# Maxima of the row scores put into a row by VectorE's 32x32 transposes instead of TensorE's transpose and ScalarE's copy

## The chip, the cores and the metric

One core of a Trainium2 chip runs the whole program. The metric is the device time of one launch in microseconds (us), given as the median of several runs; beside it there is one profiled execution, whose trace the rows below come from.

## The reference

A layer with x of 8 x 256 tokens and 512 channels. Cut to what matters here:

```
xn = layernorm(x)
c_q, c_kv = xn @ Wq_down, xn @ Wkv_down              # 64 latent columns
q_c, k_c, v_c = (c_q @ Wq_up, c_kv @ Wk_up, c_kv @ Wv_up), 128 heads of 4
q_r, k_r = xn @ Wq_rope (128 heads of 64), xn @ Wk_rope (64, shared by the heads)
scores = (q_c . k_c + q_r . k_r) / sqrt(68)          # per batch and head, 256 x 256
s = (softmax(scores) @ v_c) @ Wo
g = silu(ffn(xn))                                    # low-rank feed-forward net
out = x + s * g
```

## The kernel before

The program has three stages: projections of the input (`project_inputs`), attention (`attention`) and the end with the feed-forward net (`finish`). Each engine has a program of its own; the order of work on each is written out by hand, and semaphores tie the engines together.

The attention stage runs over 16 groups of heads (G2); a group has STEPS = 16 steps, four pairs of batches (NBP) times four launches of two heads (NS). Group 0 and group 15 are written out, the 14 between are a loop (`groups`). Each engine's `body(at, k)` holds what it does in step k, for steps that lie several places apart in the pipeline:

- `project` (L999, TensorE) makes the rope part of the queries of step k in the PSUM tile pj; ScalarE copies its rounded high part into slot1 (L848), VectorE subtracts to get the low part into slot2 (L916, once per head of the pair: it reads pj at partition 0 and then at 64, and writes slot2 at 64) and copies the rest of slot2 (L920, written at partition 0).
- `row_scores` (L985, TensorE) computes scores of step k - 1 with queries on the partitions, into the PSUM tile sx, in two halves, one per head; after each half VectorE takes the maxima over the keys (`maxima`, L906) into mx, four columns each. After two steps 16 columns of mx are full.
- The maxima are needed as a row: they enter the real scores as one more row of the contraction, slot1[KC]. So every second step (odd k) `transpose_maxima` (L952, TensorE) transposes the 16 columns into the PSUM tile sx, ScalarE copies them to mrow (L864), and SyncE moves mrow into slot1 by DMA (`max_rows`, L713).
- `scores` (L968, TensorE) computes the scores of step k - 4 and k - 3 with keys on the partitions, into st; ScalarE takes the exponentials (L887) into probs; `values` (L944) multiplies them with the values, in 32-column tiles of TensorE, for two steps at a time in every odd step.

SyncE's queue issues, in an odd step, first the row (L713, after a wait on mrow_ready) and then the content of step k (`load_content`: L697 and twice L701), the latent parts of queries and keys that row scores of step k read one step later. L697 waits for GpSimd's copy into k1 (L782). A wait and what is queued behind it on one engine go in the order of the code. In the last group's extra step k = 17 the transpose comes behind the last row scores, and ScalarE's queue issues the row.

TensorE's order in an odd step is: values of two steps, the transpose of the maxima, the second half of the scores of step k - 4, row scores of step k - 1 (first half), the projection of step k, row scores (second half). In an even step it is: both halves of scores of one step, row scores, the first half of the next scores, projection, row scores.

Of the kernel before, what the change touches and what calls it, by code (L numbers as in the profile page):

```python
# [30 lines left out]
NE = 13  # L31
# [31 lines left out]
class AttentionSemaphores:  # L63


    def __init__(self, sem, ct_lo, w_ready):
        self.ct_lo, self.w_ready = ct_lo, w_ready
        self.proj_done = sem("proj_done")
        self.ct_in = [sem(f"ct_in{s}") for s in range(NS)]
        self.st_done = sem("st_done")  # L70
        self.av_done = sem("av_done")
        self.o_evac = sem("o_evac")
        self.o_stored = sem("o_stored")
        self.k_ready = sem("k_ready")
        self.ql_done = sem("ql_done")


# [138 lines left out]
def project_inputs(nc, sb, sem, passed, x_tok, wq_down, wkv_down, wk_rope, a1T, a3T, wv_up, wq_up, wk_up, v_dram, c_dram, s_dram,  # L216
# [10 lines left out]
    with ctx:  # L227
# [372 lines left out]

        return sync, gpsimd, scalar, vector, tensor, store_tile, empty_tile, raise_up


def attention(nc, sb, sem, at_sems, passed, xh, xl, kc, krlh, c_in, probs, w_stage, wh, wl, wq_rope, w_staged, w_hi,
              w_ready, ident, v_dram, c_dram, o_dram, stored, c_loaded, ct_hi, ct_lo, ct_copy, pre, store_tile, empty_tile, raise_up):

# [6 lines left out]
    with ctx:  # L613
# [5 lines left out]
        vx = sb(ctx, "vx", [128, NS, 4, PH, 32])  # L619
        mx = sb(ctx, "mx", [128, 2, 16])  # L620
        mrow = sb(ctx, "mrow", [16, 2, 128], F32R)
        o_sb = sb(ctx, "o_sb", [128, S])
# [18 lines left out]
        smax_done = sem("smax_done")  # L641
        red_done = sem("red_done")
        mt_done = sem("mt_done")
        mrow_ready = sem("mrow_ready")
# [64 lines left out]
        def sync(sp, head, tail):  # L709
            def max_rows(at, k):  # L710
                p = (k // 2) % 2
                hold(sp, passed, mrow_ready, at.g * (STEPS // 2) + k // 2 + 1)
                sp.dma_start(slot1[KC:KC + 1, 2 * p:2 * p + 2, :, :, :].bitcast(F32),  # L713
                             mrow[:, p, :].bitcast(F32)).then_inc(mrow_in[p], 16)

# [55 lines left out]
        def gpsimd(pool, head, tail):  # L771
# [45 lines left out]
            def refill(g, s):  # L817

                hold(pool, passed, w_hi, g * NS + s + 1)
                nc.gpsimd.tensor_tensor(wl[:, s], w_stage[:, s % 2], wh[:, s], ALU.subtract).then_inc(w_ready, 1)  # L820

            nc.gpsimd.memset(vx[:, :, :, :, :], 0.0).then_inc(vx_filled, 1)
            pool.wait_ge(vx_filled, 1)
# [12 lines left out]
        def scalar(act, head, tail):  # L836
# [4 lines left out]
            def body(at, k):  # L841
# [14 lines left out]
                if s == 1 and at.live(k - 6):  # L856
# [3 lines left out]
                    nc.scalar.activation(o_sb[:, :], ob[:, 0, :], ACT.Copy).then_inc(o_evac, 1)  # L860
                if k % 2 and at.live(k - 3) and k - 3 < STEPS:
                    p = (k - 3) // 2
                    act.wait_ge(mt_done, at.g * (STEPS // 2) + p + 1)
                    nc.scalar.activation(mrow[:, p % 2, :], sx[0:16, 0, 0:128], ACT.Copy).then_inc(mrow_ready, 1)  # L864
                    if at.last and k > STEPS:
                        act.wait_ge(mrow_ready, at.g * (STEPS // 2) + p + 1)
                        act.dma_start(slot1[KC:KC + 1, 2 * (p % 2):2 * (p % 2) + 2, :, :, :].bitcast(F32),
                                      mrow[:, p % 2, :].bitcast(F32)).then_inc(mrow_in[p % 2], 16)
                if at.live(k - 4) and k - 4 < STEPS:
# [26 lines left out]
        def vector(dve, head, tail):  # L896
            def content_lo(parity, t):
                c = content[parity % 2]
                dve.wait_ge(ct_hi, t + 1)
                nc.vector.tensor_tensor(c[:, 2, :], c_in[64:128, :], c[:, 0, :], ALU.subtract).then_inc(ct_lo, 1)  # L900

            def maxima(at, k, half):
                p, i = (k // 2) % 2, k % 2
                dve.wait_ge(smax_done, 2 * at.step(k) + half + 1)
                lo = 8 * i + 4 * half
                nc.vector.tensor_reduce(mx[:, p, lo:lo + 4], sx[:, :, :].rearrange("p a (b k) -> p (a b) k", b=2),  # L906
                                        axis=AX.X, op=ALU.max).then_inc(red_done, 1)

            def body(at, k):
                if at.live(k - 2) and k - 2 < STEPS:  # L910
                    maxima(at, k - 2, 1)
                if at.live(k - 1) and k <= STEPS:
                    s = (k - 1) % NS
                    for e in range(PH):
                        dve.wait_ge(qh_done, 2 * at.step(k) + e - 1)
                        nc.vector.tensor_tensor(slot2[64:128, s, e, :, :],  # L916
                                                pj[64 * e:64 * e + 64, :].rearrange("p (a n) -> p a n", a=2),
                                                slot1[0:64, s, e, :, :], ALU.subtract).then_inc(ql_done, 1)
                if at.live(k - 1) and k <= STEPS:
                    nc.vector.tensor_copy(slot2[0:64, s], slot1[0:64, s]).then_inc(s2_done, 1)  # L920
                    maxima(at, k - 1, 0)
                if k % NS == 2 and k < STEPS and at.live(k + 2):
                    content_lo(k // NS + 1, at.turn(k) + 1)

            groups(dve, body, head, tail)

        def tensor(pe, head, tail):
# [21 lines left out]

            def transpose_maxima(at, k):  # L950
                pe.wait_ge(red_done, 2 * at.step(k) + 4)
                nc.tensor.transpose(sx[0:16, 0, 0:128], mx[:, (k // 2) % 2, :], ident[:, :]).then_inc(mt_done, 1)  # L952

            def scores(at, k, kt):
                s, v = k % NS, at.step(k)
                b = 2 * ((k // NS) % NBP)
                if kt == 0 and k % 2 == 0:
                    if at.first and k == 0:
                        pe.wait_ge(pre.krl_done, NC)
                        pe.wait_ge(pre.krh_copied, 16 * NC)  # L960
                    pe.wait_ge(mrow_in[s // 2], 16 * (at.turn(k) + 1))
                if at.live(k - 1):
# [9 lines left out]
            def row_scores(at, k, half):  # L972
# [3 lines left out]
                if not half:  # L976
                    pe.wait_ge(qh_done, 2 * v + 2)
                    pe.wait_ge(ct_in[s], 48 * (at.turn(k) + 1))
                    if at.first and k < 2:
                        pe.wait_ge(k_ready, k + 1)  # L980
                    if k % 2 == 0 and at.live(k - 2):
                        pe.wait_ge(mrow_ready, at.g * (STEPS // 2) + k // 2)
                for h in range(2):
# [19 lines left out]
            def body(at, k):  # L1003
# [4 lines left out]
                if k % 2 and not ending:  # L1008
                    if at.live(k - 7):
                        values(at, k - 7, 2)  # L1010
                        values(at, k - 6, 0)
                    if at.live(k - 3) and k - 3 < STEPS:
                        transpose_maxima(at, k - 3)
                if ending and k > STEPS + 1:
# [14 lines left out]
                if at.live(k - 1) and k <= STEPS:  # L1029
                    row_scores(at, k - 1, 1)  # L1030
                if ending and k == STEPS + 1:
                    transpose_maxima(at, k - 3)

# [5 lines left out]
def finish(nc, sb, at_sems, passed, sem, x_tok, xh, xl, lora, lora_raw, mk, ident, stored, s_dram, o_dram, r_dram, wo, w1qT, b1T, w3qT, b3T,  # L1039
# [504 lines left out]
    def tensor_tail(pe, k):  # L1544

        if k == 17:
            pe.wait_ge(w13_lo, 4)
            pe.wait_ge(sl_done, NC)
            pe.wait_ge(at_sems.ql_done, 2 * NS * NT)
            wide(pe, 0, 0)  # L1550

# [136 lines left out]
```

## Time and profile before

| what | us |
|---|---|
| median of 3 runs | 1972.71 (1969.94 to 1976.02) |
| profiled execution | 1970.24 |
| its span | 1968.1 |
| TensorE busy | 1932.3 |
| VectorE busy | 1391.0 |
| ScalarE busy | 1055.4 |
| GpSimd busy | 476.2 |

The attention stage takes some 1,700 us of the span. The granted clock of TensorE is 0.998 of full in the mean. To read the profile: busy time of a pipelined engine says little of what sets the end, so the timelines of single pairs of steps, where each event's start and end stand beside the others', are read along with the chain of waits.

### The profile page before, as it was taken

Reading aid. Unit: us, or ns where it says so; the run is one execution under the profiler, and the core shown is the slowest. Engines: PE = TensorE matmul, PEld = TensorE weight load, DVE = VectorE, ACT = ScalarE, POOL = GpSimd, SP = SyncE. Lnnn points to the kernel's source line nnn. Section 1 sums busy time; section 2 is a strip of 40 time slices with the busy share of each in tenths; the row PEclk is TensorE's granted clock in tenths of the full one; section 3 lists DMA queues with packets and bytes.
Section 4 is the critical chain, followed back from the end, with each engine's and each line's share of the span. In section 5 each row is a group of like instructions: output and inputs, shape, how many; then the busy total and the mean of one; then the engine's idle time right before and its main releaser. Section 6 shows DMA issues by size and latency. Waiting matters only on the chain.

```text
span 1968.1 us, 37690 instructions
## 1 busy us (share of the span) xinstructions
PE 1932.3 (98%) x12464; PEld 1504.6 (76%) x12464; DVE 1391.0 (71%) x1642; ACT 1055.4 (54%) x1542; POOL 476.2 (24%) x792
## 2 busy tenths in 40 slices
PE   7899999999999999999999999999999999998999
PEld 5777877777787777778777777877787777775676
DVE  8688767676776767676776767677776767687655
ACT  5656555555555555555555555555555555564222
POOL 5323121212212121212121222222131312112221
PEclk9999999999999999999999999999999999999999
DMA  7612111111212121212112121212121211234331
GB/s 240 206 38 59 31 41 38 38 37 34 45 27 50 28 50 25 51 28 43 34 39 40 35 40 34 43 28 50 29 46 29 49 28 37 46 82 132 107 102 54
DMA packets 132875, 107.97 MB, mean 55 GB/s; under 512 B 52350, under 2 KB 96430, under 8 KB 132766
## 3 DMA queue, kind: packets, MB, share of 16 engines
q1 hardware_dynamic: 132798, 107.38, 23.2%
q8 instruction: 26, 0.43, 0.1%
q14 instruction: 19, 0.16, 0.0%
q10 hardware_dynamic: 32, 0.01, 0.0%
HBM read 52.80 MB, written 27.26 MB: 41 GB/s over the span
## 4 chain that ended last, share of the span: by engine, by line
PE 94%; DVE 3%; SPq 1%; issue 1%; DMA 1%; ACT 0%; POOL 0%; DVEq 0%; ACTq 0%; POOLq 0%
PE pj L999 35%; PE st L968 24%; PE sx L985 12%; PE ob L944 12%; PE ap L1597 2%; PE sx L952 1%; PE yp L1631 1%; PE zp L1631 1%; PE gp L1538 1%; PE zp L1584 1%; PE gp L1563 1%; PE tp L565 0%; DVE mx L906 0%; PE gp L1539 0%; PE gp L1540 0%
## 5 line engine op out<-in xcount | busy, mean ns | idle before, releaser
L906 DVE TENSOR_REDUCE mx<-sx 128x4 f32<-128x1024 f32 x512 | 626.9, 1224 | 427.8 <-PE sx L985 410.0
L887 ACT ACTIVATE probs<-st 128x1024 f32<-128x1024 f32 x512 | 513.1, 1026 | 165.2 <-PE st L968 164.5
L848 ACT ACTIVATE slot<-pj 64x512 fp32r<-64x512 f32 x512 | 303.4, 592 | 424.0 <-PE pj L999 417.7
L782 POOL CAST k<-kc 64x512 fp32r<-64x512 f32 x256 | 168.1, 657 | 1055.1 <-PE st L968 1054.7
L968 PE MATMUL st<-slot,k 89*128 89x512 f32 x1024 | 417.8, 408 | 4.1 <-DMA slot<-mrow 4.1
L968 PE MATMUL st<-slot,krlh 128*128 128x512 f32 x1024 | 408.3, 399 | 0.0
L999 PE MATMUL pj<-xh,wh 128*128 128x512 f32 x1024 | 401.4, 392 | 0.9 <-DVE slot L916 0.8
L999 PE MATMUL pj<-xh,wl 128*128 128x512 f32 x1024 | 400.6, 391 | 0.0
L999 PE MATMUL pj<-xl,wh 128*128 128x512 f32 x1024 | 399.4, 390 | 0.0
L916 DVE TENSOR_TENSOR slot<-pj,slot 64x512 fp32r<-64x512 f32 x512 | 353.1, 690 | 17.4 <-ACT slot L848 1.3
L985 PEld LDWEIGHTS sx<-k,slot 88*128 88x128 f32 x2048 | 314.1, 190 | 50.4 <-issue 4.1
L985 PE MATMUL sx<-k,slot 88*128 88x256 f32 x2048 | 327.7, 282 | 3.5 <-DMA slot<-kx 1.3
L944 PE MATMUL ob<-probs,vx 128*32 128x256 f32 x4096 | 247.8, 382 | 1.1 <-ACT probs L887 1.1
L999 PEld LDWEIGHTS pj<-xh,wl 128*128 128x128 f32 x1024 | 192.2, 188 | 42.7
L999 PEld LDWEIGHTS pj<-xh,wh 128*128 128x128 f32 x1024 | 192.6, 188 | 38.3 <-issue 1.2
L999 PEld LDWEIGHTS pj<-xl,wh 128*128 128x128 f32 x1024 | 192.8, 188 | 38.1
L968 PEld LDWEIGHTS st<-slot,k 89*128 89x128 f32 x1024 | 196.1, 192 | 33.0 <-DMA slot<-mrow 4.6
L968 PEld LDWEIGHTS st<-slot,krlh 128*128 128x128 f32 x1024 | 195.7, 191 | 29.5
L944 PEld LDWEIGHTS ob<-probs,vx 128*32 128x32 f32 x4096 | 119.9, 109 | 85.0 <-ACT probs L887 2.3
L920 DVE CAST slot<-slot 64x1024 fp32r<-64x1024 f32 x256 | 176.6, 690 | 7.9
L820 POOL TENSOR_TENSOR wl<-w_stage,wh 128x512 fp32r<-128x512 f32 x60 | 77.2, 1287 | 57.6 <-ACT wh L892 57.6
L864 ACT ACTIVATE mrow<-sx 16x128 fp32r<-16x128 f32 x128 | 33.1, 259 | 88.1 <-PE sx L952 88.1
(180 smaller groups left out, 1300.8 us busy)
## 6 DMA issues: line engine op xcount, KB each, us to landing
w_stage<-in_Wq_rope SPq DMA_DIRECT2D x64, 256.0 KB, 3.1
c_scratch<-stage SPq DMA_DIRECT2D x32, 256.0 KB, 3.1
c_in<-c_scratch SPq DMA_DIRECT2D x128, 64.0 KB, 1.9
o_scratch<-o_sb SPq DMA_DIRECT2D x128, 64.0 KB, 2.1
k<-kc SPq DMA_DIRECT2D x128, 48.0 KB
slot<-kc SPq DMA_DIRECT2D x256, 24.0 KB
k<-kx SPq DMA_DIRECT2D x128, 48.0 KB
slot<-kx SPq DMA_DIRECT2D x256, 24.0 KB
```

What stands on the lines that cost most here:

```text
L782: nc.gpsimd.tensor_copy(k1[0:64, s, :, :].rearrange("p a n -> p (a n)"), krh[:, bp * CH:(bp + 1) * CH]).then_inc(k_ready, 1)
L820: nc.gpsimd.tensor_tensor(wl[:, s], w_stage[:, s % 2], wh[:, s], ALU.subtract).then_inc(w_ready, 1)
L848: nc.scalar.activation(slot1[0:64, (k - 1) % NS, e, :, :], pj[64 * e:64 * e + 64, :].rearrange("p (a n) -> p a n", a=2), ACT.Copy).then_in ...
L887: nc.scalar.activation(probs[:, k % NS, kt], st[:, kt], ACT.Exp, scale=SCALE).then_inc(exp_done, 1)
L906: nc.vector.tensor_reduce(mx[:, p, lo:lo + 4], sx[:, :, :].rearrange("p a (b k) -> p (a b) k", b=2), axis=AX.X, op=ALU.max).then_inc(red_d ...
L916: nc.vector.tensor_tensor(slot2[64:128, s, e, :, :], pj[64 * e:64 * e + 64, :].rearrange("p (a n) -> p a n", a=2), slot1[0:64, s, e, :, :] ...
L920: nc.vector.tensor_copy(slot2[0:64, s], slot1[0:64, s]).then_inc(s2_done, 1)
L944: last = nc.tensor.matmul(ob[j:j + 32, 0, :], vx[:, s, 2 * h + kt, e, :], probs[:, s, kt, h, e * S:(e + 1) * S], start=(s == 0 and kt == 0 ...
L968: last = nc.tensor.matmul(st[:, kt, h, :].rearrange("p (e n) -> p e n", e=PH), kk, q[0:n_rows, s, :, h, :], start=(n == 0), stop=(n == 1))
L985: last = nc.tensor.matmul(sx[:, h, qt * S:(qt + 1) * S], slot1[0:KC, s, half, h, qt * 128:qt * 128 + 128], k1[0:KC, s, h, :], start=True, ...
L999: last = nc.tensor.matmul(pj[:, :], w[:, s, c, :], xx[:, c, ts], start=(c == 0 and n == 0), stop=(c == KD - 1 and n == 2))
L1597: last = nc.tensor.matmul(ap[i % 2][:, :], o[:, k, i * 128:(i + 1) * 128], w[:, k, :], start=(k == 0 and n == 0), stop=(k == KD - 1 and n ...
```

## The change

VectorE does the turning. A function `max_row` waits for both steps' maxima and issues four transposes of 32x32 from mx (partitions 32j to 32j + 31) to mrow (partitions 0 to 31, columns from 32j), in SBUF. mx is widened to 32 columns for each of its two buffers, zeroed once by GpSimd, and of the rounded type that the copy gave the row before; mrow gets 32 partitions, of which 16 are sent. TensorE's transpose, ScalarE's copy and TensorE's wait for that copy are gone. SyncE waits for the fourth transpose. In the extra step ScalarE's queue still issues the row. Two waits are added that took their place in the order from the transpose before: TensorE waits for the last staged tile before the first scores, and for all maxima before it uses the banks in the last stage.

```diff
-        mx = sb(ctx, "mx", [128, 2, 16])
-        mrow = sb(ctx, "mrow", [16, 2, 128], F32R)
+        mx = sb(ctx, "mx", [128, 2, 32], F32R)
+        mrow = sb(ctx, "mrow", [32, 2, 128])
...
             def max_rows(at, k):
                 p = (k // 2) % 2
-                hold(sp, passed, mrow_ready, at.g * (STEPS // 2) + k // 2 + 1)
+                hold(sp, passed, mrow_ready, 4 * (at.g * (STEPS // 2) + k // 2 + 1))
                 sp.dma_start(slot1[KC:KC + 1, 2 * p:2 * p + 2, :, :, :].bitcast(F32),
-                             mrow[:, p, :].bitcast(F32)).then_inc(mrow_in[p], 16)
+                             mrow[0:16, p, :]).then_inc(mrow_in[p], 16)
...
+            nc.gpsimd.memset(mx[:, :, :].bitcast(F32), 0.0).then_inc(mx_zeroed, 1)
             nc.gpsimd.memset(vx[:, :, :, :, :], 0.0).then_inc(vx_filled, 1)
...
-                if k % 2 and at.live(k - 3) and k - 3 < STEPS:
+                if at.last and k == STEPS + 1:
                     p = (k - 3) // 2
-                    act.wait_ge(mt_done, at.g * (STEPS // 2) + p + 1)
-                    nc.scalar.activation(mrow[:, p % 2, :], sx[0:16, 0, 0:128], ACT.Copy).then_inc(mrow_ready, 1)
...
+            def max_row(at, k):
+
+                dve.wait_ge(red_done, 2 * at.step(k) + 4)
+                for j in range(4):
+                    nc.vector.transpose(mrow[:, (k // 2) % 2, 32 * j:32 * j + 32],
+                                        mx[32 * j:32 * j + 32, (k // 2) % 2, :].bitcast(F32)).then_inc(mrow_ready, 1)
+
             def body(at, k):
                 if at.live(k - 2) and k - 2 < STEPS:
                     maxima(at, k - 2, 1)
+                if k == STEPS + 1:
+                    max_row(at, k - 3)
...
                                                 slot1[0:64, s, e, :, :], ALU.subtract).then_inc(ql_done, 1)
+                if k % 2 and at.live(k - 3) and k < STEPS:
+                    max_row(at, k - 3)
                 if at.live(k - 1) and k <= STEPS:
                     nc.vector.tensor_copy(slot2[0:64, s], slot1[0:64, s]).then_inc(s2_done, 1)
...
-            def transpose_maxima(at, k):
-                pe.wait_ge(red_done, 2 * at.step(k) + 4)
-                nc.tensor.transpose(sx[0:16, 0, 0:128], mx[:, (k // 2) % 2, :], ident[:, :]).then_inc(mt_done, 1)
...
+                        wait_tile(pe, NC * NE - 1)
...
-                    if k % 2 == 0 and at.live(k - 2):
-                        pe.wait_ge(mrow_ready, at.g * (STEPS // 2) + k // 2)
...
+            pe.wait_ge(at_sems.red_done, 2 * NS * NT)
```

On TensorE, in an odd step of the loop (ob is the values' tile, st the scores', sx the row scores'), before:

```order
L944 MATMUL ob<-probs,vx 32x256 [waits vx_ready,exp_done]
L944 MATMUL ob<-probs,vx 32x256 x15
L951 ISA
L952 MATMUL sx<-ident,mx 16x128 [waits red_done]
L968 MATMUL st<-slot,k 128x512 [waits exp_done]
L968 MATMUL st<-slot,krlh 128x512
```

and with the change:

```order
L956 MATMUL ob<-probs,vx 32x256 [waits vx_ready,exp_done]
L956 MATMUL ob<-probs,vx 32x256 x15
L977 MATMUL st<-slot,k 128x512 [waits exp_done]
L977 MATMUL st<-slot,krlh 128x512
L977 MATMUL st<-slot,k 128x512
```

The transpose is gone, and scores follow the values directly.

On VectorE, in an odd step of the loop (the slot of the subtractions and of the copy is slot2), before:

```order
L906 TENSOR_REDUCE mx<-sx 128x4 [waits smax_done]
L915 ISA
L916 TENSOR_TENSOR slot<-pj,slot 64x512 [waits qh_done] x2
L920 COPY slot<-slot 64x1024
L904 REGISTER_ALU
L906 TENSOR_REDUCE mx<-sx 128x4 [waits smax_done]
```

and with the change:

```order
L907 TENSOR_REDUCE mx<-sx 128x4 [waits smax_done]
L925 ISA
L926 TENSOR_TENSOR slot<-pj,slot 64x512 [waits qh_done] x2
L912 REGISTER_ALU
L914 STREAM_TRANSPOSE mrow<-mx 32x32 [waits red_done]
L914 STREAM_TRANSPOSE mrow<-mx 32x32 x3
L932 COPY slot<-slot 64x1024
```

Four transposes stand between the subtractions and the copy; the maxima that the first of them waits for are the ones ahead of the subtractions.

## Rows read from the trace of the kernel before

**Rows 1.** page, busy time of each engine, share of the span, instructions

```profile
PE 1932.3 (98%) x12464; PEld 1504.6 (76%) x12464; DVE 1391.0 (71%) x1642; ACT 1055.4 (54%) x1542; POOL 476.2 (24%) x792
```

**Rows 2.** chain of waits, 937 to 951 us: start us, us, engine and tile

```profile
937.21 0.21 PE sx L952
...
941.57 0.48 PE sx L985 x4
...
950.45 0.21 PE sx L952
```

**Rows 3.** timeline of TensorE: start us, us, engine, line, operation

```profile
937.14 0.28 PE L952 MATMUL sx<-ident,mx 128*16 128x128 f32 x1
...
937.49 0.40 PE L968 MATMUL st<-slot,krlh 128*128 128x512 f32 x1
...
1784.05 1.07 PE L944 MATMUL ob<-probs,vx 128*32 128x256 f32 x16
1785.05 0.50 PE L968 MATMUL st<-slot,k 89*128 89x512 f32 x1
1785.39 0.40 PE L968 MATMUL st<-slot,krlh 128*128 128x512 f32 x1
```

**Rows 4.** timelines of ScalarE, GpSimd and SyncE's queue (SPq)

```profile
937.46 0.27 ACT L864 ACTIVATE mrow<-sx 16x128 fp32r<-16x128 f32 x1 [1.34 <-PE sx L952]
...
937.83 0.59 SPq L713 DMA_DIRECT2D slot<-mrow  x1
...
938.54 0.70 POOL L782 CAST k<-kc 64x512 fp32r<-64x512 f32 x1 [2.43 <-PE st L968]
...
939.35 0.80 SPq L697 DMA_DIRECT2D k<-kc  x1
...
1708.24 0.61 SPq L713 DMA_DIRECT2D slot<-mrow  x1
1708.97 0.80 SPq L697 DMA_DIRECT2D k<-kx  x1
```

**Rows 5.** timeline of VectorE

```profile
1.52 0.17 DVE L519 TENSOR_REDUCE mk<-ident 128x1 f32<-128x16 f32 x1 [1.52 <-POOL ident L362]
...
7.46 0.38 DVE L470 BATCH_NORM_AGGREGATE mv<-stats 128x2 f32<-128x6 f32 x4
...
936.64 1.41 DVE L916 TENSOR_TENSOR slot<-pj,slot 64x512 fp32r<-64x512 f32 x2
938.08 0.69 DVE L920 CAST slot<-slot 64x1024 fp32r<-64x1024 f32 x1
938.88 1.23 DVE L906 TENSOR_REDUCE mx<-sx 128x4 f32<-128x1024 f32 x1
```

**Rows 6.** two lines of VectorE: duration ns minimum, median, maximum

```profile
L916 DVE TENSOR_TENSOR slot<-pj,slot x512: 683/690/697, 76.8 to 1767.2; 64x512 fp32r<-64x512 f32 x171
...
L470 DVE BATCH_NORM_AGGREGATE mv<-stats x16: 148/150/184, 7.5 to 50.7; 128x2 f32<-128x6 f32 x16
```

**Rows 7.** timeline of TensorE and its weight loads (PEld)

```profile
931.00 0.39 PE L968 MATMUL st<-slot,k 89*128 89x512 f32 x1
...
943.58 0.61 PEld L985 LDWEIGHTS sx<-k,slot 88*128 88x128 f32 x4
...
944.24 0.40 PE L968 MATMUL st<-slot,k 89*128 89x512 f32 x1
...
1740.01 0.54 PEld L985 LDWEIGHTS sx<-k,slot 88*128 88x128 f32 x4 [0.48 <-issue]
...
1740.59 0.40 PE L968 MATMUL st<-slot,k 89*128 89x512 f32 x1
```

**Rows 8.** stretches: us, busy of PE, PEld, DVE, ACT, POOL, clock, DMA share, GB/s

```profile
929.65:929.70 0.05, 0.05 (x2) 0.05 (x1) 0.05 (x1) 0.00 (x0) 0.00 (x0) 1.00 0.14 41
...
1739.50:1739.55 0.05, 0.05 (x1) 0.03 (x1) 0.05 (x1) 0.05 (x1) 0.00 (x0) 1.00 0.10 41
```

**Rows 9.** what TensorE's transpose (L952) waited for: us, times

```profile
  DVE mx L906: 8.6, 10
```

More of the change, by code:

```diff
@@ L75, in __init__ @@
         self.ql_done = sem("ql_done")
+        self.red_done = sem("red_done")
 def hold(eng, passed, semaphore, value):
@@ L599, in tensor @@
                     raise_up(pe, c, n)
-        return sync, gpsimd, scalar, vector, tensor, store_tile, empty_tile, raise_up
+        return sync, gpsimd, scalar, vector, tensor, store_tile, empty_tile, raise_up, wait_tile
 def attention(nc, sb, sem, at_sems, passed, xh, xl, kc, krlh, c_in, probs, w_stage, wh, wl, wq_rope, w_staged, w_hi,
-              w_ready, ident, v_dram, c_dram, o_dram, stored, c_loaded, ct_hi, ct_lo, ct_copy, pre, store_tile, empty_tile, raise_up):
+              w_ready, ident, v_dram, c_dram, o_dram, stored, c_loaded, ct_hi, ct_lo, ct_copy, pre, store_tile, empty_tile, raise_up, wait_tile):
     KC = 64 + 3 * HD * PH
@@ L641, in attention @@
         smax_done = sem("smax_done")
-        red_done = sem("red_done")
-        mt_done = sem("mt_done")
+        red_done = at_sems.red_done
+        mx_zeroed = sem("mx_zeroed")
         mrow_ready = sem("mrow_ready")
@@ L860, in body @@
                     nc.scalar.activation(o_sb[:, :], ob[:, 0, :], ACT.Copy).then_inc(o_evac, 1)
-                if k % 2 and at.live(k - 3) and k - 3 < STEPS:
+                if at.last and k == STEPS + 1:
                     p = (k - 3) // 2
-                    act.wait_ge(mt_done, at.g * (STEPS // 2) + p + 1)
-                    nc.scalar.activation(mrow[:, p % 2, :], sx[0:16, 0, 0:128], ACT.Copy).then_inc(mrow_ready, 1)
[L865 to L868, printed above, removed]
+                    act.wait_ge(mrow_ready, 4 * (at.g * (STEPS // 2) + p + 1))
+                    act.dma_start(slot1[KC:KC + 1, 2 * (p % 2):2 * (p % 2) + 2, :, :, :].bitcast(F32),
+                                  mrow[0:16, p % 2, :]).then_inc(mrow_in[p % 2], 16)
                 if at.live(k - 4) and k - 4 < STEPS:
@@ L903, in maxima @@
                 p, i = (k // 2) % 2, k % 2
+                if at.first and k == 0:
+                    dve.wait_ge(mx_zeroed, 1)
                 dve.wait_ge(smax_done, 2 * at.step(k) + half + 1)
@@ L1011, in body @@
                         values(at, k - 6, 0)
-                    if at.live(k - 3) and k - 3 < STEPS:
-                        transpose_maxima(at, k - 3)
                 if ending and k > STEPS + 1:
@@ L1030, in body @@
                     row_scores(at, k - 1, 1)
-                if ending and k == STEPS + 1:
-                    transpose_maxima(at, k - 3)
             groups(pe, body, head, tail)
```

## The prediction

> **What bounds the kernel now.** I read the page's busy shares first: TensorE is busy for 98% of the span, VectorE for 71% [rows 1]. The chain of waits gives the transpose of the maxima 0.21 us in each pair of steps [rows 2]. I then read one pair on every engine, because a queue that is off the chain can hold a margin that no total shows. A pair takes 13.24 us (937.21 to 950.45 [rows 2]), and there are 128 (16 groups of 16 steps). The reader should see in the timelines which event ends last before each TensorE group: mostly TensorE's own work, but with hardly anything spare at one place, the content that SyncE issues right behind the row (mrow).
>
> **TensorE: the transpose and its slot.** In the pair at 937 us the transpose starts at 937.14, right behind the column-tiled value matmuls, and the second score matmul starts at 937.49, 0.35 us later. At the program's end a value group of the same kind is followed by a score group with no transpose between: first score matmul 1785.05, second 1785.39, 0.34 us later [rows 3]. So the slot is no gain: the transpose's short weight load and its columns run where the first score matmul would otherwise stand waiting for its 128 columns of weights. I take 0.01 us a pair, over 120 pairs **-1.2 us**. The bounds are that 0.01 and the chain's 0.21. The Trainium skill has a rule for the gap itself (TensorEngine Tiling (Array Packing), Key Properties): a change of tiling mode drains TensorE. By it the gap belongs to the value matmuls and stays, and the trace agrees with its 0.34 us.
>
> **ScalarE.** The copy of the row goes (0.27 us [rows 4]). ScalarE is not on the path between maxima and scores at that place: its next work waits for score matmuls. Nothing is gained. If that cover were gone, 0.27 us a pair would be.
>
> **VectorE: four transposes.** They stand between the two subtractions (L916) and the copy (L920), in odd steps. No row shows such a transpose. The length of one: a reduction of 128x16 takes 0.17 us [rows 5]; 16 more columns at the pace of VectorE's long rows (690 ns for 512 columns less 170 ns for 16, over 496: about 1.05 ns a column) give 0.19 us. Lower end 0.15 (the 128x6 aggregation, 150 ns), upper end 0.22 (0.19 plus 32 columns once more, should the block be filled before it is emptied). The pitch: four aggregations in a row take 0.38 us where one takes 0.150, so they overlap by about 0.07 each. Two L916 take 1.41 us at 690 ns each, so they don't overlap but lie 0.03 us apart [rows 5, 6]. What differs: the aggregations all start at partition 0, while L916 reads its PSUM tile at partition 0 and then at 64, and L920 behind it goes back to an output at partition 0 and starts 0.03 us after the end (936.64 + 1.41 = 938.05, then 938.08). The four transposes read mx at partitions 0, 32, 64, 96 in turn, so I price them as L916: 4 x 0.19 + 3 x 0.03 = **0.85 us** from the first's start to the last's end. Ends: 4 x 0.15 + 0.09 = 0.69 and 4 x 0.22 + 0.09 = 0.97. If they overlap as the aggregations do: 4 x (0.19 - 0.07) + 0.07 = 0.55. The Trainium skill states this as a rule (VectorE: DVE Perf Modes, Two Vector instructions with no wait between them): an instruction whose operand starts in another group of 32 partitions than the one used before is held, and "starts only when every earlier Vector instruction has finished". The rows of L916 and L920 agree with it; the rule speaks against this change.
>
> TensorE waits next for VectorE at the second row scores (941.57 [rows 2]), behind 12 projection matmuls that start as before, since the subtractions keep their place. The maxima for them now end at 938.88 + 1.23 = 940.11; with 0.85 + 0.03 more in the queue, and no wait for matmuls left before them, they start at 938.08 + 0.88 + 0.69 + 0.03 = 939.68 and end at 940.91. The projection hides the four; if that cover were gone, all of 0.88 us a pair would be on the path.
>
> **SyncE's queue: what the later row pushes.** The row is now stored with the fourth transpose. Before: ScalarE's copy ends at 937.73 and SyncE issues the row at 937.83, 0.10 us later; the next issue (L697, content of step k) then waits until GpSimd's copy ends at 939.24 and starts at 939.35 [rows 4]. Now: transposes from 938.08 to 938.93, issue at 939.03. A row and a content issue back to back start 0.73 us apart (1708.24 to 1708.97), so L697 comes at 939.76: **0.41 us late**. The three content issues, their DMAs and what waits for them all move with it. The limit on the transposes for no delay here is 0.85 - 0.41 = 0.44 us.
>
> Who waits for the content: row scores of step k, in the next step. Does it have 0.41 us to spare? In the tail, content issued at 1735.78 comes last: its final packets are at 1739.55, the weight load goes at 1740.01 (0.46 later), and the score matmul behind the four row scores at 1740.59, 0.58 after that [rows 7, 8]. In the pair at 937 us the weight load goes at 943.58; next to matmuls that start in steps of 0.23 us it is not early, and the matmul behind is at 944.24. Late content at 943.58 would give 944.16, so 0.08 us is spare. Moved by 0.41: 943.99 + 0.58 = 944.57, **0.33 us lost**. In the pair before it the last packet is at 929.70 and the matmul behind at 931.00: 929.70 + 0.46 + 0.41 + 0.58 = 931.15, **0.15 us lost** [rows 7, 8]. The two kinds alternate; the mean is 0.24, over 120 pairs **+28.8 us**. 128 pairs exist; the ones in which the queue is busy with loads of the last stage are left out.
>
> **Head and tail.** In the first steps TensorE waits at the transpose for the maxima, 8.6 us in 10 waits of the whole run [rows 9], the bound of that gain; most of it returns at the projection, which waits for the subtractions behind the same maxima. At the end VectorE's queue is the chain, and two calls of 0.85 us stand in it, +1.7 us at most; the last one takes the place of the transpose and the copy (0.28 + 0.27). I take both together as 0. The zeroing of mx on GpSimd (once) and the wait for the last staged tile before the first scores come long before they are needed.
>
> **The sum.** -1.2 + 28.8 = +27.6 us. The profiled execution took 1970.24 us for a span of 1968.1; with the sum 1997.8. The median of the runs lies 2.5 us above the profiled execution, so I forecast 2000.3 us. With 0.69 us for the four the delay is 0.25: 0.17 and 0.00 us lost, mean 0.085, +10 us: 1982. With 0.97 the delay is 0.53: 0.45 and 0.27, mean 0.36, +43 us: 2015.
>
> **The rivals.**
> - *Hidden after all.* The transposes overlap (0.55 us): the delay is 0.11, of which 0.08 is spare in one kind and more in the other, 0.02 us a pair in the mean: about 1972.7 - 1.2 + 2 = 1973.5 us. For it: the aggregations. Against it: L916, L920. Likewise if content lands sooner once its issue is not tied to GpSimd. Chance 0.20.
> - *Faster: the slot is worth something.* If the drain vanished with the transpose, each pair would win between 0.01 and 0.21 us; it decides for a gain as soon as the delay of the queue is under 0.08 us, which asks for transposes under 0.52 us. At 0.11 us x 128 the time is 1958.6 us. The Trainium skill (TensorE: Matmul & The Clock Gate, PE-mode transpose) puts such a transpose at about 275 ns in a kernel's context, and the row has 0.28; by that figure the removal would give 128 x 0.275 = 35 us. Against it stand the two distances of 0.35 and 0.34 us. Chance 0.07.
> - *Much slower: a transpose costs as much as an operation of 256 columns.* Half of L916's 0.69 us, 0.35, gives 4 x 0.35 + 0.09 = 1.49 us, a delay of 1.05 and 0.88 us a pair: 2077 us. Nothing in the rows for it but that the form is unknown. Chance 0.05.
>
> **The numbers.** A measurement of this kernel can tell 0.3%, 5.9 us, from no change. My forecast has 0.68. It is slower by over 5.9 us in all of its range. With the third rival slower is 0.73, from which I move 0.01 for a sum near the bound: 0.72. Same has the first rival and a little of the others, 0.22; faster 0.06. The range: the forecast's own is 1982 to 2015; for 8 in 10 it must reach the first rival, so it goes down to 1970.
>
> **What would show it.** Right: four transposes of about 0.19 us, each starting 0.03 us after the last; SyncE issues the row 0.10 us after the fourth and content 0.73 us behind that; the weight load of the row scores in even steps shows idle time that ends with the landing of content; the pair grows from 13.24 to about 13.47 us; first to second score matmul 0.34 us. Wrong: transposes that overlap; content still issued 0.1 us after GpSimd's copy; a pair of 13.1 us or less; a new wait at the second row scores, or at the scores for the row itself.

## The result, and the profile after

The changed kernel takes **2018.6 us** (median of 4 runs, 2017.08 to 2019.04) against 1973.07 us (1969.94 to 1976.02) for the kernel before, now with a fourth run: a ratio of **1.023** (95% interval 1.0215 to 1.0248), 45.5 us slower. The forecast was 2000.3 us, slower, with a range from 1970 to 2015. The direction and the mechanism were right; the loss was 45.5 us instead of 27.6, and the time lies outside the range. The profiled execution took 2018.73 us for a span of 2016.6.

The page of the changed kernel: busy shares (line 1 answers to [rows 1]), the chain by engine, and the group of the new transposes:

```profile
PE 1959.7 (97%) x12336; PEld 1496.5 (74%) x12336; DVE 1490.7 (74%) x2154; ACT 1027.8 (51%) x1414; POOL 523.4 (26%) x793
...
PE 65%; DVE 11%; DMA 9%; SPq 8%; issue 7%; ACT 1%; DVEq 0%; ACTq 0%
...
L914 DVE STREAM_TRANSPOSE mrow<-mx 32x32 f32<-32x32 f32 x512 | 102.8, 201 | 15.9
```

VectorE gained 99.7 us of busy time, close to the 102.8 us of the transposes. TensorE is still at 97%, a share that says nothing of the cause. The second line does: in the chain that ended last, SyncE's queue now has 8% and the DMAs 9%. Before the change the same line of the page was

```profile
PE 94%; DVE 3%; SPq 1%; issue 1%; DMA 1%; ACT 0%; POOL 0%; DVEq 0%; ACTq 0%; POOLq 0%
```

The chain through one odd step and into the next, in the loop (start, length, what):

```profile
963.22 0.21 DVE mrow L914
963.47 0.05 issue
963.51 0.59 SPq L714
...
964.30 0.80 SPq L698
965.10 0.05 issue
965.15 0.68 SPq L702
965.83 0.04 issue
965.87 2.58 DMA slot<-kc
968.46 0.14 issue
968.59 0.71 PE sx L992 x4
```

Read it downwards: the fourth transpose (the others stand ahead of it in the chain), issue of the row, issue of the content right behind, its DMA, and then the row scores of the next step. That is the path the prediction named. The row's own DMA isn't in it.

Two pairs of steps side by side. The timelines of TensorE (matmuls, then weight loads), where each x32 row is a pair's start:

```profile
932.50 1.93 PE L956 MATMUL ob<-probs,vx 128*32 128x256 f32 x32
946.15 1.93 PE L956 MATMUL ob<-probs,vx 128*32 128x256 f32 x32
948.01 0.50 PE L977 MATMUL st<-slot,k 89*128 89x512 f32 x1
948.35 0.40 PE L977 MATMUL st<-slot,krlh 128*128 128x512 f32 x1
...
955.44 0.40 PE L977 MATMUL st<-slot,k 89*128 89x512 f32 x1
```

```profile
941.29 0.54 PEld L992 LDWEIGHTS sx<-k,slot 88*128 88x128 f32 x4 [0.60 <-DMA slot<-kx]
...
954.86 0.54 PEld L992 LDWEIGHTS sx<-k,slot 88*128 88x128 f32 x4 [0.53 <-issue]
```

and those of VectorE, then of SyncE's queue:

```profile
947.51 1.41 DVE L926 TENSOR_TENSOR slot<-pj,slot 64x512 fp32r<-64x512 f32 x2
948.95 0.89 DVE L914 STREAM_TRANSPOSE mrow<-mx 32x32 f32<-32x32 f32 x4
949.87 0.69 DVE L932 CAST slot<-slot 64x1024 fp32r<-64x1024 f32 x1
```

```profile
936.30 0.59 SPq L714 DMA_DIRECT2D slot<-mrow  x1
937.08 0.81 SPq L698 DMA_DIRECT2D k<-kx  x1
...
949.94 0.57 SPq L714 DMA_DIRECT2D slot<-mrow  x1
950.70 0.75 SPq L698 DMA_DIRECT2D k<-kc  x1
```

The transposes run from 948.95 to 949.84, 2.80 to 3.69 us after the pair's start. The row is issued at 949.94, the content at 950.70, 4.55 us after the start; in the pair before, 4.58 (937.08 - 932.50). Before the change it was 4.07: content at 939.35 [rows 4], in the pair that starts at 935.28 (timeline of the kernel before, TensorE):

```profile
935.28 1.93 PE L944 MATMUL ob<-probs,vx 128*32 128x256 f32 x32
```

The weight load of the even step's row scores now ends an idle time of 0.53 to 0.60 us, where [rows 7] show one at 943.58 that starts in step. The load at 954.86 has the next score matmul behind it at 955.44, 0.58 us later as in the prediction, and first and second score matmul are 0.34 us apart (948.01, 948.35), with no transpose ahead of them. The mean pair between 300 and 1650 us, from the starts of the first and the last value group there over their number (about 100), grew from **13.234 to 13.604 us** (forecast about 13.47): 0.370 x 128 = 47 us, against 48.5 us of span (2016.6 less 1968.1). The time is lost evenly in the loop.

### The profile page after: what moved, and what is told of

Its sections match the earlier page's. It is cut to its first block, busy times and chain, and to the rows that moved or that the text cites. A ratio compares the mean times of both kernels' runs of the same rounds, so it can differ in the third digit from the quotient of the medians.

```text
span 2016.6 us, 37584 instructions
## 1 busy us (share of the span) xinstructions
PE 1959.7 (97%) x12336; PEld 1496.5 (74%) x12336; DVE 1490.7 (74%) x2154; ACT 1027.8 (51%) x1414; POOL 523.4 (26%) x793
## 4 chain that ended last, share of the span: by engine, by line
PE 65%; DVE 11%; DMA 9%; SPq 8%; issue 7%; ACT 1%; DVEq 0%; ACTq 0%
PE pj L1006 25%; PE st L977 15%; PE sx L992 10%; PE ob L956 5%; DVE slot L926 5%; DMA slot<-kx 4%; DMA slot<-kc 4%; SPq L698 3%; DVE mrow L914 2%; SPq L702 2%; PE ap L1601 2%; SPq L714 2%; DVE mx L907 1%; PE yp L1635 1%; PE zp L1635 1%
## 5 line engine op out<-in xcount | busy, mean ns | idle before, releaser
L907 DVE TENSOR_REDUCE mx<-sx 128x4 fp32r<-128x1024 f32 x512 | 626.9, 1224 | 339.4 <-PE sx L992 331.1
L783 POOL CAST k<-kc 64x512 fp32r<-64x512 f32 x256 | 155.7, 608 | 1039.9 <-PE st L977 1039.5
L992 PEld LDWEIGHTS sx<-k,slot 88*128 88x128 f32 x2048 | 305.1, 190 | 109.7 <-issue 63.9
L992 PE MATMUL sx<-k,slot 88*128 88x256 f32 x2048 | 337.5, 287 | 25.6 <-DMA slot<-kc 8.6
L802 POOL COPY vx<-v_it 128x32 f32<-128x32 f32 x256 | 112.0, 438 | 22.9 <-POOL kc L816 8.9
L914 DVE STREAM_TRANSPOSE mrow<-mx 32x32 f32<-32x32 f32 x512 | 102.8, 201 | 15.9
```

The costliest lines, as they stand in the source:

```text
L783: nc.gpsimd.tensor_copy(k1[0:64, s, :, :].rearrange("p a n -> p (a n)"), krh[:, bp * CH:(bp + 1) * CH]).then_inc(k_ready, 1)
L802: nc.gpsimd.tensor_copy(vx[:, s, :, :, 4 * s:4 * s + 4], v_it[:, (kk // NS) % 2].rearrange("p n (e s r) -> p n e s r", e=PH, s=NS)[:, :, : ...
L914: nc.vector.transpose(mrow[:, (k // 2) % 2, 32 * j:32 * j + 32], mx[32 * j:32 * j + 32, (k // 2) % 2, :].bitcast(F32)).then_inc(mrow_ready, 1)
L992: last = nc.tensor.matmul(sx[:, h, qt * S:(qt + 1) * S], slot1[0:KC, s, half, h, qt * 128:qt * 128 + 128], k1[0:KC, s, h, :], start=True, ...
```

## The experiments

Each kernel is the changed one with the edit shown, unless it says otherwise, and is compared with the kernel before on the same chip (1970.5 us for three, two, same_part and row_on_act; 1970.7 for load_alone, slot_alone and first; 1969.7 for copy_first and act_again). Times after the start of a pair are from the timelines of five pairs (880 to 1010 us); pairs are means as above.

**Fewer transposes.** Three, and then two; mrow is zeroed once, and the rest of the row stays zero. ScalarE's wait in the extra step is lowered likewise.

```diff
-                hold(sp, passed, mrow_ready, 4 * (at.g * (STEPS // 2) + k // 2 + 1))
+                hold(sp, passed, mrow_ready, 3 * (at.g * (STEPS // 2) + k // 2 + 1))
...
+            nc.gpsimd.memset(mrow[:, :, :], 0.0).then_inc(mx_zeroed, 1)
...
-                for j in range(4):
+                for j in range(3):
...
```

> Three transposes instead of four (the last 32 queries' maxima are left out of the row, which keeps zeros there). Theory (the row comes late by the length of the transposes, and SyncE issues the content behind it): three take 3 x 0.20 + 2 x 0.03 = 0.66 us instead of the 0.89 of the changed kernel, the content's delay falls from 0.50 to 0.27 us, the loss of a pair from about 0.41 to 0.18 us: about 1995 us. Rival (each transpose costs the path its own time, wherever it stands): three quarters of 45.5 us are left: 2007 us.

> Two transposes instead of four (half of the maxima are left out of the row). Theory: 0.43 us in a row, a delay of 0.04 us, which is spare in both kinds of pair: within 3 us of the kernel before, about 1973 us. Rival (each transpose costs the path its own time): half of 45.5 us is left, 1996 us.

The edit shown is that of three; two has 2 in place of 3. Three: 1989.2 us, ratio 1.0095 (1.0076 to 1.0113). Two: 1967.5 us, 0.9986 (0.9974 to 0.9997). Two transposes cost nothing that can be measured, the third 22 us, the fourth 29 us (2018.6 less 1989.2; 27 us by the two ratios, as the change was measured beside another set of runs of the kernel before). That is a limit, not a load: the content is issued 4.10, 4.33 and 4.56 us after the pair's start with two, three and four, and the pair takes 13.206, 13.373 and 13.604 us. Both versions came out about 6 us under what I expected. Of that, 2.6 us is the kernel before, which ran at 1970.5 us here and at 1973.07 beside the change; most of the rest is the slot of TensorE's transpose, 4.4 us by the run slot_alone below, which the expectations hardly counted. Fewer transposes did not lower VectorE's busy time: 1490 us with three and 1492 with two, against 1491 with four, because its copy into slot2 starts earlier and then takes longer (last section). So the time of the program falls here while VectorE's load stays.

**The same number, but overlapping (same_part).** All four read the first block of mx, so that they take the same number of instructions, semaphores and columns but never change the partitions they read.

```diff
-                                        mx[32 * j:32 * j + 32, (k // 2) % 2, :].bitcast(F32)).then_inc(mrow_ready, 1)
+                                        mx[0:32, (k // 2) % 2, :].bitcast(F32)).then_inc(mrow_ready, 1)
```

> All four transposes read mx at partitions 0 to 31, so that the row holds the first 32 queries' maxima four times. Theory (they stand one behind the other because each reads at another group of partitions than the one before): now they overlap by 0.07 to 0.08 us each, four take 4 x 0.12 + 0.08 = 0.56 us, the content's delay is 0.17 us and the loss of a pair about 0.08 us: about 1983 us. Rival (a transpose never overlaps with the next, whatever it reads): four still take 0.89 us and the time stays at 2018 us.

2000.2 us, ratio 1.0145 (1.0126 to 1.0163), faster than the change by about 18 us, but 17 us above my figure. The line's own durations (min/median/max ns), then one pair on VectorE, GpSimd and SyncE:

```profile
L914 DVE STREAM_TRANSPOSE mrow<-mx x512: 156/157/200, 90.3 to 1802.5; 32x32 f32<-32x32 f32 x171
```

```profile
953.82 0.48 DVE L914 STREAM_TRANSPOSE mrow<-mx 32x32 f32<-32x32 f32 x4
954.23 0.64 DVE L932 CAST slot<-slot 64x1024 fp32r<-64x1024 f32 x1
...
954.25 1.10 POOL L783 CAST k<-kc 64x512 fp32r<-64x512 f32 x1 [2.39 <-PE st L977]
...
954.39 0.59 SPq L714 DMA_DIRECT2D slot<-mrow  x1
955.45 0.81 SPq L698 DMA_DIRECT2D k<-kc  x1
```

Four transposes in 0.48 us: the first of four takes 200 ns, the others 157, and each of these starts 0.06 us before the end of the one ahead; the copy behind starts 0.07 us before they end. So the 0.89 us of the change comes from the partitions it reads. The Trainium skill (VectorE: DVE Perf Modes, Two Vector instructions with no wait between them) says that an instruction whose operand starts in another group of 32 partitions than the one used before is held until all earlier ones have finished; here the trace agrees, with 0.03 us between two transposes in the change and an overlap of 0.06 us in this kernel. The surprise is in the last rows. The row is issued 0.42 us earlier than in the change, yet the content only 0.12 us (4.44 against 4.56 us after the pair's start): it waits for GpSimd's copy into k1, which took 1.10 us instead of 0.61 and ended at 955.35, 0.48 us after VectorE's copy (954.87). With the transposes short, that copy of VectorE's falls onto GpSimd's. This kernel has a second reason for late content, and its pair still fits the first: content at 4.44, pair 13.476.

**VectorE's load without the wait (load_alone).** The kernel before, with four transposes of a spare tile at the place of the new ones; nobody waits for them.

```diff
+            nc.gpsimd.memset(spare[:, :], 0.0)
...
+                if k % 2 and at.live(k - 3) and k < STEPS:
...
+                    for j in range(4):
+                        nc.vector.transpose(spare_row[:, 32 * j:32 * j + 32], spare[32 * j:32 * j + 32, :])
```

> The kernel before, with four further transposes of a spare tile on VectorE at the place where the change has them; nobody waits for them. Theory (VectorE's load as such is hidden): TensorE waits for VectorE only behind the projection, within 3 us of the kernel before. Rival (the four transposes hold up TensorE through the second maxima, or take a port from GpSimd): slower, up to the 45.5 us of the change.

1970.0 us, ratio 0.9998 (0.9989 to 1.0007); the pair is 13.238 us. Transposes of 0.2 us, 508 of them, cost nothing on VectorE, later copy and later second maxima included. They take 0.84 us for four and not 0.89, with 0.01 us between two and not 0.03; the content is issued 3.97 us after the pair's start.

**The slot alone (slot_alone).** The kernel before without TensorE's transpose, except in the last step; ScalarE waits for the maxima instead and copies what lies in sx.

```diff
-                    act.wait_ge(mt_done, at.g * (STEPS // 2) + p + 1)
...
+                        act.wait_ge(red_done, 2 * at.step(k - 3) + 4)
...
-                    if at.live(k - 3) and k - 3 < STEPS:
-                        transpose_maxima(at, k - 3)
```

> The kernel before without TensorE's transpose in all steps but the last (ScalarE copies what stands in the row scores' tile, so that the row is not the maxima). Theory (the slot of the transpose is filled by the weight load that the first score matmul would wait for anyway): 0.01 us a pair, 1 to 2 us in all, not to be told from no change; the second score matmul still comes 0.34 us after the start of the first. Rival (the slot is worth its columns, 0.11 us, or the 0.21 us of the chain): 14 to 27 us faster, 1946 to 1959 us.

1965.8 us, ratio 0.9976 (0.9967 to 0.9984), 4.8 us faster. From the value group to the row scores the kernel before takes 2.92 us (timeline, TensorE):

```profile
948.52 1.93 PE L944 MATMUL ob<-probs,vx 128*32 128x256 f32 x32
...
951.44 0.64 PE L985 MATMUL sx<-k,slot 88*128 88x256 f32 x4
```

and this kernel 2.90, with 0.34 us between first and second score matmul (947.06 - 946.72), as in the change:

```profile
944.86 1.93 PE L947 MATMUL ob<-probs,vx 128*32 128x256 f32 x32
...
946.72 0.50 PE L971 MATMUL st<-slot,k 89*128 89x512 f32 x1
947.06 0.40 PE L971 MATMUL st<-slot,krlh 128*128 128x512 f32 x1
...
947.76 0.63 PE L988 MATMUL sx<-k,slot 88*128 88x256 f32 x4
```

The pair is 13.200 us, 0.034 us shorter. So the slot is worth 0.034 x 128 = 4.4 us: more than my 0.01 a pair, and an eighth of the 0.28 us its row shows. The Trainium skill (TensorE: Matmul & The Clock Gate, PE-mode transpose) gives about 275 ns for a transpose on TensorE in one kernel's context, beside a figure for 128x128 bf16; this one has 16 columns of four bytes, and its row shows 0.28 us. Taken as a saving, that would have been 35 us in this run; it isn't.

**The row on another queue (row_on_act, and again as act_again).** All of the change, but in every odd step ScalarE's queue issues the row, and SyncE's queue issues content only.

```diff
-                if k % 2 and at.live(k - 3) and not (at.last and k > STEPS):
-                    max_rows(at, k - 3)
...
-                if at.last and k == STEPS + 1:
+                if k % 2 and at.live(k - 3) and k - 3 < STEPS:
                     p = (k - 3) // 2
```

> ScalarE's queue issues the row in every odd step, SyncE's queue no longer waits for it. The transposes stay. Theory (the loss is all in SyncE's queue behind the row): content goes right behind GpSimd's copy again, the pair takes 13.24 us and the program about 1972 us, at most 5 us more should ScalarE's issue of about 0.6 us delay an exponential that TensorE waits for. Rival (VectorE's longer work holds up TensorE): the time stays near 2018 us.

1966.5 us, ratio 0.998 (0.997 to 0.999). The whole loss is gone, with the four transposes in place at 0.90 us. The row itself is issued hardly sooner, 3.73 us after the pair's start against 3.80, so its own lateness isn't what cost the time. This is also the only version with a full row that ended below the kernel before, so it was run a second time:

> The change with the row issued by ScalarE's queue in every odd step, the same kernel as row_on_act, over more rounds: it is the version that may beat both. Theory A expects 1965 to 1967 us, a ratio to the kernel before of 0.997 to 0.998: the four transposes cost nothing once the content's issue is not behind the row, and the slot of TensorE's transpose gives back 0.03 us a pair, 4.4 us. The rival (the earlier result was scatter between the rounds) expects 1.000.

1967.7 us (11 runs, 1964.11 to 1968.96), ratio **0.9986 (0.9977 to 0.9995)**: faster by 1.0 to 4.5 us, less than the 0.3% that I had taken as the bound of what counts. What SyncE waited for between 250 and 1650 us, what TensorE's weight loads did, and the two queues in one pair (start of the pair 948.53):

```profile
SPq L83 <- POOL k L781: 646.7, 212, 3.8
```

```profile
PEld st L975 <- issue: 44.0, 107, 0.4
```

```profile
952.26 0.51 ACTq L864 DMA_DIRECT2D slot<-mrow  x1
...
952.48 0.74 SPq L698 DMA_DIRECT2D k<-kx  x1
```

Content goes at 3.95 us after the start, right behind GpSimd's copy, and the weight loads of the row scores have no idle time left. The one that remains, 0.4 us before the scores (st), lies behind the value group; before the change it stood there too, ahead of the transpose. In the changed kernel the same view has three rows. The first and third are where the loss sits: 59 us in which the weight loads stand still, of which about 41 us (103 pairs, each 0.40 us longer than here) lengthened the program:

```profile
PEld sx L992 <- issue: 51.3, 90, 0.7
PEld st L977 <- issue: 42.4, 103, 0.4
PEld sx L992 <- DMA slot<-kx: 7.9, 13, 0.6
```

**The transposes earlier (first).** Between the maxima and the subtractions, so that the row is out long before the content.

```diff
-                if k == STEPS + 1:
+                if k % 2 and at.live(k - 3) and k - 3 < STEPS:
                     max_row(at, k - 3)
...
-                if k % 2 and at.live(k - 3) and k < STEPS:
-                    max_row(at, k - 3)
```

> The changed kernel with the transposes ahead of the subtractions instead of behind them. Theory: the row is ready 1.44 us earlier, before SyncE needs it, so the content is no longer late; but the subtractions end 0.92 us later, and the projection, which starts about 0.6 us after their end before the change, waits some 0.35 us in every odd step. That costs 120 x 0.35 = 42 us: about 2014 us, by another wait (the projection on the subtractions). Rival (the loss has to do with VectorE's transposes and not with what is queued behind the row): the same time and the same wait on content as in the changed kernel.

2034.8 us, ratio 1.0328 (1.0313 to 1.0343), the wrong place by more than I thought. Content is early (3.94), but the subtractions end at 3.70 instead of 2.77 and the projection waits for them:

```profile
PE pj L1004 <- DVE slot L926: 22.4, 102, 0.2
```

The projection starts at 3.75 instead of 3.37 and ends 0.51 us later, the pair is 13.718 us, 0.52 over 13.20. Of the 0.51, 0.38 is the later start. Of the other 0.13, 0.10 lies between its first two matmuls (944.48 and 944.81 in one pair: 0.33 us instead of 0.23), whose first weight load had waited as well and started together with its matmul. I had expected only a later start, 0.35 us over 120 pairs; against the kernel before, the pair grew by 0.48 us, over 128.

**The transposes later (copy_first).** Behind VectorE's copy, a test at the far end of the rule that the runs above give: the pair is 13.20 us plus whatever the content is issued later than 4.15.

```diff
+                if at.live(k - 1) and k <= STEPS:
+                    nc.vector.tensor_copy(slot2[0:64, s], slot1[0:64, s]).then_inc(s2_done, 1)
                 if k % 2 and at.live(k - 3) and k < STEPS:
                     max_row(at, k - 3)
                 if at.live(k - 1) and k <= STEPS:
-                    nc.vector.tensor_copy(slot2[0:64, s], slot1[0:64, s]).then_inc(s2_done, 1)
                     maxima(at, k - 1, 0)
```

> The change, but VectorE does the copy into slot2 (0.69 us) first and the four transposes behind it. Theory A (the loss per pair is the lateness of the content issue, one for one, counted from 4.15 us after the start of the value matmuls, on a pair of 13.20 us; slope and edge read from the runs with two, three and four transposes and with transposes that overlap): the transposes run from 3.52 to 4.42, the row is issued at 4.52, content at 5.29; the pair grows by 1.14 to 14.34 us, about 2110 us in all (1.14 x 128 = 146 over 1965). Theory B (VectorE's load or its own order costs the time, not the queue): the same instructions in another order on an engine with idle time, about 2020 us as the change. Theory C (beside it): GpSimd cannot work while VectorE's copy runs; its copy into k1 in odd steps then ends at 3.95 as before the change, with 0.70 us, and not at 3.85 with 0.61, and its copy into vx returns from 0.69 to 0.20 us.

2093.5 us, ratio 1.063 (1.0614 to 1.0647). One pair, from VectorE, GpSimd and SyncE; its value matmuls start at 939.49:

```profile
942.29 0.69 DVE L930 CAST slot<-slot 64x1024 fp32r<-64x1024 f32 x1
942.90 0.89 DVE L914 STREAM_TRANSPOSE mrow<-mx 32x32 f32<-32x32 f32 x4
...
942.73 0.72 POOL L783 CAST k<-kc 64x512 fp32r<-64x512 f32 x1 [2.45 <-PE st L978]
...
943.88 0.58 SPq L714 DMA_DIRECT2D slot<-mrow  x1
944.66 0.81 SPq L698 DMA_DIRECT2D k<-kc  x1
```

Content at 5.17, pair 14.200. The rule gives 13.20 + 5.17 - 4.15 = 14.22. I had put the content at 5.29, because I let the transposes begin after the end of VectorE's copy; they begin 0.08 us before it. So my 14.34 and 2110 us were too high, and the rule itself held. Put together, for the kernels without TensorE's transpose (first isn't among them, since there the projection sets the pair):

| kernel | content issued after the pair's start | pair | content - 4.15 | pair - 13.20 |
|---|---|---|---|---|
| act_again | 3.95 | 13.202 | below 0 | 0.00 |
| two | 4.10 | 13.206 | below 0 | 0.01 |
| three | 4.33 | 13.373 | 0.18 | 0.17 |
| same_part | 4.44 | 13.476 | 0.29 | 0.28 |
| after | 4.56 | 13.604 | 0.41 | 0.40 |
| copy_first | 5.17 | 14.200 | 1.02 | 1.00 |

The two figures of the rule, 4.15 and 13.20, were read from the runs with two, three and four transposes, from same_part and from row_on_act; the test is copy_first. Over a microsecond, and for two different reasons of lateness, the pair pays one for one. VectorE's busy time doesn't order this table: 1491 us in after and in act_again, 1480 in copy_first.

## Why the prediction was right or wrong

**The step that failed: the size of the loss behind the late content, +28.8 us.** It was 0.24 us a pair over 120 pairs in the prediction and 0.37 over 128, or 47 us, in the run. Three readings in it were short: the distance between the issues of row and content, the spare time in every other pair, and the number of pairs. The range then let only the length of the transposes vary, so it ended at 2015.

**What bounds, and the path: right.** Transposes, row, content behind it in SyncE's queue, weight load of the row scores. The row on the other queue takes the path away and the whole loss with it; the load alone costs nothing, as forecast for the copy and the second maxima (cover held).

**Four transposes: 0.85 us forecast, 0.89 measured.** Each takes 0.20 us instead of 0.19, 0.03 apart as forecast; priced like the subtractions, rightly, since same_part shows the other case at 0.48. I had 0.55 for that case, so the first rival ("hidden after all") fell with its condition.

**SyncE: 0.41 us late forecast, 0.50 measured (failed).** The row went 0.10 us after the fourth transpose, as forecast. Content followed it by 0.76 to 0.79 us instead of 0.73, which I had taken from one pair of issues in the tail. With the transposes' 0.04 that is 4.48 forecast and 4.55 or 4.58 measured.

**The spare time: 0.08 and 0.26 us forecast, 0.06 and 0.20 measured (failed, in the second kind).** In the mean of every other pair of the loop, the kind at 937 us grew from 13.22 to 13.67 us, so 0.45 of 0.51 was paid (0.33 forecast). The other kind grew by 0.29 of 0.49 (0.15 forecast). For that kind I added 0.46 us to the last packet at 929.70 [rows 8] and so put the load 4.07 us behind the content issue of 926.09; where the load does wait for it, the distance is 4.16 in the pair shown (950.70 to 954.86) and 4.13 in the mean. That error of 0.06 went straight into the loss. An event that has slack doesn't show its own limit; I estimated it from a third place, the tail.

**The slot: 0.01 us a pair forecast, 0.034 measured alone, none of it kept.** The gap of 0.34 us stays when the transpose goes, as forecast. That it comes from the change of tiling is not shown: the run first has 0.33 us between the first two projection matmuls, with no value group ahead of them. What both places share is that the first weight load starts together with its matmul, as the prediction had it too. In the changed kernel the content sets the start of the row scores, so a slot that ends 0.03 us sooner only makes the content 0.03 later against it; the growth from 13.234 already holds that.

**The number of pairs: 120 forecast, 128 right.** Growth of a pair times 128 gives 47 us, 1 us off the span's 48.5. There was no ground to leave out the pairs in which SyncE also loads for the last stage.

**The sum.** Forecast: 0.24 x 120 - 1.2 = 27.6. Measured: 0.09 more lateness and 0.04 less spare make 0.37; over 120 pairs +15.6, eight more pairs +3.0, no slot gain +1.2: 47.4. The figure at the upper end of my range (0.97 us of transposes, a delay of 0.53 us, +43 us) is near what happened, but by luck: the transposes took 0.89 us, and other terms made up the rest. The range held the price of the transposes open and kept the issue distance and the spare time as exact; each had been read from one place. Head and tail at 0 held within 2 us.

**The rivals.** Hidden: no. Faster by the slot: the slot's own value is 4.4 us, not 14 (0.11 x 128) or 35. That it decides once the delay is under the spare time was right: with the queue's delay under the spare time, as in act_again, the change is slightly faster. Much slower: no, 0.20 us and not 0.35.

## What to carry to other kernels

When an operation moves to an engine with free time, ask in which queue its result is then waited for, and what stands behind that wait; here a row that nobody needed for microseconds held back the transfers that were needed first, and sending it from another queue removed all 45 us. Where the cost is lateness minus spare time, an error of 0.05 us in either is a large part of the answer and is multiplied by every iteration: read both at several places and put each one's spread into the range. The busy share of an engine neither warned of this nor showed it afterwards; the row "idle before, released by" of the weight loads did.

## What the runs showed of the hardware

**Copies of VectorE and of GpSimd from SBUF to SBUF hold each other up, and the one that starts first goes first.** In same_part the two copies start together (954.25 and 954.23) and GpSimd's takes 1.10 us instead of 0.61. In the changed kernel the small copy into vx, 0.20 us alone, meets the same copy of VectorE (949.87 to 950.56); the timeline of GpSimd:

```profile
949.38 0.61 POOL L783 CAST k<-kc 64x512 fp32r<-64x512 f32 x1 [3.35 <-PE st L977]
949.94 0.69 POOL L802 COPY vx<-v_it 128x32 f32<-128x32 f32 x1
```

It ends at 950.63, just behind VectorE's. With VectorE's copy at its old place (copy_first) the vx copy is back at 0.20 us and the one into k1 at 0.72, with its end at 943.45, 0.47 behind VectorE's end at 942.98. Where GpSimd starts first, VectorE waits: in the run two its copy into slot2 takes 1.13 us instead of 0.69, on VectorE and GpSimd:

```profile
938.88 1.13 DVE L933 CAST slot<-slot 64x1024 fp32r<-64x1024 f32 x1
```

```profile
938.85 0.61 POOL L783 CAST k<-kc 64x512 fp32r<-64x512 f32 x1 [2.41 <-PE st L978]
```

The Trainium skill has it (SBUF — State Buffer, Who interferes with whom): a copy of VectorE's in a mode that uses both port pairs contends with GpSimd, whoever issues first gets the shared pair for the whole instruction, and the other "fully blocks". The trace agrees, but for some 0.13 us of each GpSimd copy that runs in the meantime (0.48 us of 0.61 are left in same_part when VectorE ends). The transposes don't do this: in the changed kernel GpSimd's copy into k1 (949.38) runs beside the last two of them in 0.61 us. So the change even freed that copy (3.85 us after the pair's start instead of 3.96), which SyncE's order then hid.

**A 32x32 transpose of four-byte elements on VectorE** takes 157 ns, and starts 0.06 us before the end of the one ahead, when it reads from the same 32 partitions as that one; it takes 200 ns, and starts 0.03 us after that end, when it reads from another 32 (0.01 us in load_alone, where nothing is signalled). For four: 0.48 against 0.89 us.
